# Loading all rows of the key stacks before the query stacks, for the first half of the next batch, on the SyncE queue

## The chip, the cores and the metric

The kernel runs on one core of one Trainium2 chip. The metric is device time in microseconds (us) of one execution. Three runs of the kernel before gave 1634.35, 1639.19 and 1637.96 us; their median is 1637.96. TensorE is PE here, VectorE is DVE, ScalarE is ACT, GpSimd is POOL, and SyncE is SP; SP issues nearly all DMAs.

## The reference, cut to what matters

The program is one decoder layer over 8 batches of 512 tokens of width 256, with a context of 1601 rows per batch. It has three parts, each followed by a residual sum and a layer norm. The change touches only how the operands of the second part reach their place.

```python
x = layernorm(x + self_attention_3_iterations(x))
# cross attention, 16 heads of 16 dims, 1601 context rows
q = split_heads(x @ Wq.T); k = split_heads(ctx @ Wk.T); v = split_heads(ctx @ Wv.T)
scores = einsum('bhqd,bhkd->bhqk', q, k) / sqrt(16)
scores = where(mem_mask, scores, -inf)
attn = softmax(scores, axis=-1)
x = layernorm(x + merge_heads(attn @ v) @ Wo.T)
# adapter FFN: one of 8 adapters is chosen per batch
base = x @ W_base + b_base
h = relu(x @ W_enc + b_enc); recon = h @ W_dec + b_dec
top1 = argmin(mean((recon - x) ** 2))
x = layernorm(x + base + relu(x @ W_down[top1] + b_down[top1]) @ W_up[top1] + b_up[top1])
```

## The kernel before, in words

After a front part the kernel runs one software pipeline. A batch has 4 groups of 4 heads (groups are numbered through, `m` = 4b to 4b+3 for batch b), and a group has 13 slots, one for each 128 context rows: 52 slots per batch, numbered 0 to 51. In a slot PE computes four score tiles (`pe_scores`, L1129), the product of the previous slot's probabilities with the values (`pe_values`, L1148), two pair tiles of scores for row maxima of a later group (`pe_pair`, L1089), and part of a projection job for the batch before or after (`pe_job`). ACT takes exponentials (L1267). DVE reduces the pair tiles to maxima (`dve_pair`, L1452 and L1455), evacuates jobs, and does small steps that the table `VECTOR_WORK` assigns to slots. The pair tiles have a ring of two buffers, so PE can write a pair only when DVE has read the pair two before it. Every engine works through its list in order.

The score product is made of bf16 parts. Queries and keys are split in three bf16 parts each, which are written to DRAM (`parts_dram`, `key_parts_dram`) and loaded back as stacks of 16-row blocks. Six blocks make the contraction: the three top ones (j = 0 to 2) and the three low ones (j = 3 to 5), each for two parities, so a "top" or a "low" load is 6 DMAs. The maxima of pair tiles use the top rows only and wait for the semaphore `stacked`; the full scores need the low rows too and wait for `stacked_low`. A key stack DMA moves 200.1 KB, a query stack DMA 64 KB.

The stacks hold two halves (c = 0: groups 0 and 1 of a batch; c = 1: groups 2 and 3). The half c = 0 of the next batch is loaded in the middle of the present one, after slot 25, when the scores of group 4b+1 are done: `sp_stacks(nxt, 0, m + 1)` in `sp_batch`. Seven batches do this (nxt = 1 to 7). The first user of the new top rows is a pair tile of slot 35; the first user of the low rows is slot 0 of the next batch.

Between the stacks lies `sp_spread_inverses(between)` for group 4b+1. It waits for DVE's reciprocal of the softmax sums, writes it to DRAM (L1653), waits for that write to land (L1656), and loads it back spread over 64 partitions (L1657) into `err`. In slot 33 DVE multiplies the outputs by it (the step `scale`, L1345), after a wait on the semaphore `spread`. DVE has its next pair tiles, `xk_rest` of the job `kproj` 5 (L1399) and the maxima of group 4b+3 behind that step; PE needs the pair buffers, and in slot 35 the job `loss` (L1039) waits for that `xk_rest`. The maxima go through DRAM as well (`sp_max_rows`, L1621 and L1627) and are needed by the first score of slot 39.

Of the kernel before, what the change touches and what calls it, by code (L numbers as in the profile page):

```python
# [714 lines left out]
def cross_attention_and_ffn(nc, g):  # L715

    sem, W, ident, ident_b, scores, pairs, av = g.sem, g.W, g.ident, g.ident_b, g.scores, g.max_scores, g.av
    with ExitStack() as s:
# [858 lines left out]
        def sp_key_parts_out(n):  # L1577

            for one in on["kparts_out"]:
                nc.sync.wait_ge(one, 48 * n)  # L1580
# [6 lines left out]
        def stack_row(j, par):  # L1587
            return ROW_A[par] + HD * j if j < TOP else ROW_B[par] + HD * (j - TOP)

        def sp_key_stacks(b, c, top, some=slice(0, S2)):  # L1590

            for j in range(TOP) if top else range(TOP, len(KPART)):
                src = g.kpart_dram[c, KPART[j]][:, some].rearrange("(h e d) n -> e d h n", e=2, d=HD)
                for par in range(2):
                    row = stack_row(j, par)
                    nc.sync.dma_start(kst[row:row + HD, c, :, par, some],
                                      src[par]).then_inc(on["stacked"] if top else on["stacked_low"], 16)
            if top and some.start == 0:
                for par in range(2):
                    row = R_MASK[par]  # L1600
                    nc.sync.dma_start(kst[row:row + 1, c, :, par, :],
                                      g.mask_dram[b:b + 1].unsqueeze(1).broadcast_to([1, HP, SP_])).then_inc(on["stacked"], 16)

        def sp_query_stacks(c, top, some=slice(0, T), done=None):
            for j in range(TOP) if top else range(TOP, len(QPART)):
                src = g.part_dram[c, QPART[j]][:, some].rearrange("(h e d) n -> e d h n", e=2, d=HD)
                for par in range(2):
                    row = stack_row(j, par)
                    nc.sync.dma_start(qst[row:row + HD, c, :, par, some],
                                      src[par]).then_inc(done or (on["stacked"] if top else on["stacked_low"]), 16)  # L1610
# [35 lines left out]
        def sp_spread_inverses(m):  # L1646

            sp = nc.sync
            k, these = half_rows(m)
            sp.wait_ge(inverted, m + 1)  # L1650
            if m >= 2:
                sp.wait_ge(spread, 16 * (m - 1))
            sp.dma_start(g.rsum_dram[m % 2].rearrange("j (s x) -> (j s) x", x=GH * T // P), rs[:, m % 2, :]).then_inc(rs_out, 16)  # L1653
            sp.wait_ge(rs_out, 16 * (m + 1))
            if m >= 2:
                sp.wait_ge(scaled, m - 1)  # L1656
            sp.dma_start(rsb[these, :], g.rsum_dram[m % 2].unsqueeze(1).broadcast_to([GH, HD, T])).then_inc(spread, 16)  # L1657

        def sp_stacks(b, c, between=None):

            if b:
                sp_key_parts_out(2 * (b - 1) + 1 + c)
                if c:
                    nc.sync.wait_ge(on["qparts_out"], 48 * (2 * (b - 1) + 1 + c))
            if b or c:
                before = GROUPS * b - (NG if c == 0 else 0)
                if before:
                    nc.sync.wait_ge(made, GH * XKT * before)
            if b and not c:
                sp_key_stacks(b, c, True)  # L1670
                nc.sync.wait_ge(on["qparts_out"], 48 * (2 * (b - 1) + 1 + c))
                sp_query_stacks(c, True)
                if between is not None:
                    sp_spread_inverses(between)
                sp_query_stacks(c, False)
                sp_key_stacks(b, c, False)
                return
            for top in (True, False):
                sp_query_stacks(c, top)
                if top and between is not None:  # L1680
                    sp_spread_inverses(between)
                sp_key_stacks(b, c, top)
# [30 lines left out]
        def sp_batch(b):  # L1713
# [6 lines left out]
            if prev >= 0:  # L1720
                sp_move_outputs(m - 1)
                sp_load_x1(prev)
            sp_stacks(b, 1, m - 1 if prev >= 0 else None)
            if nxt < B:
                if b:
# [16 lines left out]
            if nxt < B:  # L1742
                sp_stacks(nxt, 0, m + 1)
                sp_free_key_dram(nxt, 1)
                sp_key_parts(4, use + 4)
                if nxt + 1 < B:
                    sp_load_x(nxt + 1)
                sp_key_parts(5, use + 5)
            else:
                sp_spread_inverses(m + 1)  # L1750
# [659 lines left out]
```

## Time and profile before

| | |
|---|---|
| median of three runs | 1637.96 us (1634.35 to 1639.19) |
| the profiled execution | 1639.14 us, span 1636.6 us |
| mean granted PE clock | 0.992 |
| PE busy | 1577.6 us, 96% of the span |
| DVE busy | 1287.8 us, 79% |
| ACT busy | 1044.5 us, 64% |
| SP's DMA queue (q1) | 38.1% of 16 engines, 123.06 MB |

One batch takes about 187 us in the steady part (the same ACT step of the chain stands at 536.14 and at 723.40 us). The profiled execution is 2.5 us longer than its span, and 1.2 us longer than the median. The queue of DMAs is far from full over the whole span, but it is worked in bursts: the DMA line of the page goes from 0 to 7 tenths from slice to slice. Times of rows are from the start of the span.

### The profile page before, as it was taken

The page shows a single profiled execution, that of the slowest core. Times are in us where ns is not written, and L with a number is a line of the kernel's source. Part 1 is how long each engine was busy: PE and PEld are TensorE (multiplying, and loading weights), DVE is VectorE, ACT ScalarE, POOL GpSimd, SP SyncE. Part 2 cuts the span into 40 slices and gives each one's busy share as a digit, 9 for nine tenths or more (in the row PEclk, how much of TensorE's full clock was granted, in tenths as well). Part 3 has the DMA queues.
Part 4 walks back from the last instruction along what each step waited for, and adds up shares of the span by engine and source line. Part 5 has one row for each costly group of instructions (what it writes and reads, how often), then busy time and mean ns, then how long its engine had stood idle before and what let it go on. Part 6 is the DMA issues. An engine that isn't in the chain of part 4 may idle for free.

```text
span 1636.6 us, 25498 instructions
## 1 busy us (share of the span) xinstructions
PE 1577.6 (96%) x9560; PEld 582.7 (36%) x9560; DVE 1287.8 (79%) x1905; ACT 1044.5 (64%) x1984; POOL 162.5 (10%) x153
## 2 busy tenths in 40 slices
PE   6778999999999999999999999999999999999997
PEld 5442323332333333332334323432333323332234
DVE  5788887888789878888788877888778877887523
ACT  2226777766666676776666666666666676666661
POOL 6311000100011000100001000100001000000000
PEclk9889999999999999999999999999999999999999
DMA  5556162543417171452607152261707234160010
GB/s 157 114 137 107 60 96 54 94 108 55 98 28 140 48 119 33 84 131 36 113 16 140 63 89 64 65 115 49 128 11 117 57 55 84 50 79 5 10 33 16
DMA packets 118664, 125.21 MB, mean 77 GB/s; under 512 B 35187, under 2 KB 100340, under 8 KB 118541
## 3 DMA queue, kind: packets, MB, share of 16 engines
q1 hardware_dynamic: 117724, 123.06, 38.1%
q8 instruction: 75, 1.23, 0.3%
q10 hardware_dynamic: 816, 0.53, 0.1%
q14 instruction: 49, 0.39, 0.1%
HBM read 84.18 MB, written 35.03 MB: 73 GB/s over the span
## 4 chain that ended last, share of the span: by engine, by line
PE 88%; DVE 5%; ACT 4%; DMA 2%; issue 1%; POOL 1%; SPq 0%; POOLq 0%; DVEq 0%
PE banks L1129 24%; PE values L1148 24%; PE banks L1089 12%; PE work L1019 5%; PE work L1005 5%; PE work L964 4%; PE work L1026 3%; ACT xprobs L1267 3%; PE work L1032 3%; DVE xneg_max_pieces L1452 2%; PE work L1011 2%; PE work L1035 1%; DMA max_dram<-xneg_max_rows 1%; PE work L1044 1%; PE work L949 1%
## 5 line engine op out<-in xcount | busy, mean ns | idle before, releaser
L1267 ACT ACTIVATE xprobs<-banks 128x512 f32<-128x512 f32 x1664 | 900.6, 595 | 407.9 <-PE banks L1129 403.9
L1452 DVE TENSOR_REDUCE xneg_max_pieces<-banks 128x2 f32<-128x1024 f32 x768 | 908.5, 1218 | 209.4 <-PE banks L1089 205.6
L1129 PE MATMUL banks<-xq_stacks,xk_stacks 99*128 99x512 bf16 (+1 forms) x1664 | 518.4, 385 | 11.4 <-ACT xprobs L1267 3.5
L1148 PE MATMUL values<-xprobs,xv_rows 128*17 128x512 f32 x3328 | 437.9, 598 | 1.6 <-ACT xprobs L1267 1.6
L1129 PEld LDWEIGHTS banks<-xq_stacks,xk_stacks 99*128 99x128 bf16 (+1 forms) x1664 | 127.3, 97 | 394.9 <-ACT xprobs L1267 285.7
L1089 PE MATMUL banks<-xk_stacks,xq_stacks 49*128 49x512 bf16 (+1 forms) x2048 | 251.3, 335 | 13.9 <-DVE xneg_max_pieces L1452 11.6
L1089 PEld LDWEIGHTS banks<-xk_stacks,xq_stacks 49*128 49x128 bf16 x2048 | 57.5, 94 | 344.7 <-DVE xneg_max_pieces L1452 226.2
L1148 PEld LDWEIGHTS values<-xprobs,xv_rows 128*17 128x17 f32 x3328 | 55.1, 95 | 124.4 <-issue 118.8
L1523 POOL TENSOR_TENSOR xk_parts<-xk_rest,xk_parts 128x401 bf16<-128x401 f32 (+1 forms) x64 | 59.1, 923 | 376.3 <-ACT xk_parts L1246 376.3
L1518 POOL TENSOR_TENSOR xrstd<-xrstd,mhalf 128x4 f32<-128x4 f32 x21 | 21.2, 1012 | 594.4 <-DVE xrstd L1321 594.4
L1019 PE MATMUL work<-xvT,ctxT_a 128*128 128x128 f32 (+1 forms) x416 | 56.8, 281 | 2.0 <-DVE xk_rest L1399 1.9
L1019 PEld LDWEIGHTS work<-xvT,ctxT_a 128*128 128x128 f32 (+1 forms) x416 | 54.8, 193 | 10.9 <-issue 3.9
L1455 DVE TENSOR_REDUCE xneg_max_pieces<-banks 128x8 f32<-128x520 f32 x64 | 44.5, 695 | 17.6 <-PE banks L1089 17.4
L1026 PE MATMUL work<-x2T,wenc 128*128 128x512 f32 x112 | 57.8, 596 | 0.0
L1230 ACT ACTIVATE xk_parts<-work 128x401 bf16<-128x401 f32 (+1 forms) x64 | 32.5, 507 | 39.6 <-PE work L1005 39.6
L1528 POOL TENSOR_TENSOR xq_parts<-xq_rest,xq_parts 128x512 bf16<-128x512 f32 x15 | 17.4, 1157 | 405.4 <-ACT xq_parts L1249 405.4
L1019 PEld LDWEIGHTS work<-xvT,ctxT_b 128*128 128x128 f32 (+1 forms) x416 | 54.4, 187 | 8.7 <-ACT x2T L1192 0.8
L1032 PE MATMUL work<-x2T,wdecT 128*128 128x512 f32 x112 | 57.2, 591 | 0.0
L1019 PE MATMUL work<-xvT,ctxT_b 128*128 128x128 f32 (+1 forms) x416 | 55.4, 274 | 0.0
L1005 PE MATMUL work<-ctxT_a,xkT 128*128 128x400 f32 (+1 forms) x128 | 52.2, 528 | 0.8 <-DVE xq_rest L1413 0.8
L1337 DVE STREAM_TRANSPOSE xT<-xa 32x256 f32<-32x256 f32 x112 | 48.8, 435 | 3.3
L1005 PE MATMUL work<-ctxT_b,xkT 128*128 128x400 f32 (+1 forms) x128 | 48.2, 498 | 0.0
(299 smaller groups left out, 1040.7 us busy)
## 6 DMA issues: line engine op xcount, KB each, us to landing
xk_stacks<-key_parts_dram SPq DMA_DIRECT2D x186, 200.1 KB, 10.3
key_parts_dram<-xk_parts SPq DMA_DIRECT2D x144, 100.0 KB, 2.1
xq_stacks<-parts_dram SPq DMA_DIRECT2D x186, 64.0 KB, 5.9
ctxT_a<-in_ctxT SPq DMA_DIRECT2D x4, 1601.0 KB, 7.7
ctxT_b<-in_ctxT SPq DMA_DIRECT2D x4, 1601.0 KB, 8.0
parts_dram<-xq_parts SPq DMA_DIRECT2D x45, 128.0 KB, 1.8
key_parts_dram<-xk_parts SPq DMA_DIRECT2D x48, 100.2 KB, 9.5
xa<-in_x SPq DMA_DIRECT2D x8, 512.0 KB, 8.9
```

The costliest lines, as they stand in the source:

```text
L964: last = nc.tensor.matmul(W[:, i * D:(i + 1) * D], left, right, start=c == 0, stop=c == steps - 1)
L1005: last = pe.matmul(W[:, 0:n], xkT[:, kin, c * P:(c + 1) * P], ctx[b % 2][:, kin, k0:k0 + n], start=kin == 0, stop=kin == CH - 1)
L1019: last = pe.matmul(W[0:rows, (tt - first) * P:(tt - first + 1) * P], ctx[b % 2][:, kin, tt * P:tt * P + rows], xvT[:, kin, c * P:(c + 1) * P],
L1026: last = pe.matmul(W[:], wenc[:, kin, 2 * i:2 * i + 2, :].rearrange("p n h -> p (n h)"), x2T[:, kin, :], start=kin == 0, stop=kin == CH - 1)
L1032: last = pe.matmul(W[:], wdecT[:, kin, i * P:(i + 1) * P], x2T[:, kin, :], start=kin == 0, stop=False)
L1089: last = pe.matmul(pairs[n % MRING][:, par, at:at + w], qst[rows, k, h2, par, q * P:(q + 1) * P], kst[rows, k, h2, par, k0:k0 + w], start= ...
L1129: pe.matmul(at, kst[0:ROWS[par], k, h2, par, t * P:(t + 1) * P], qst[0:ROWS[par], k, h2, par, :], start=True, stop=True).then_inc(made, 1)
L1148: last = pe.matmul(av[32 * j:32 * j + HD + 1, :], vals[:, k, t, gr * GH + j, :], probs[:, sl % 2, j, :], start=t == 0, stop=t == XKT - 1)
L1267: nc.scalar.activation(probs[:, sl % 2, j, :], score_bank(n)[0], ACT.Exp).then_inc(exped, 1)
L1337: v.transpose(xT[32 * c:32 * (c + 1), :, :].rearrange("p k (n a i) -> p a k n i", a=P // 32, i=32)[:, a], xa[32 * a:32 * (a + 1), :, :].re ...
L1452: nc.vector.tensor_reduce(nmp[:, of % 2, :, j2, q, piece], pairs[n % MRING][:, :, :], AX.X, ALU.max, negate=True).then_inc(on["mxr"], 1)
L1523: nc.gpsimd.tensor_tensor(kpart[:, i % KBUF, 2, 0:n], krest[:, i % KBUF, 0:n], kpart[:, i % KBUF, 1, 0:n], ALU.subtract).then_inc(on["klow ...
```

## The change

In the branch of `sp_stacks` for the first half of the next batch, the six DMAs of the low key rows move from the end to the place behind the top key rows and the mask rows. They are now issued before the wait for the query parts, the top query rows, the inverses and the low query rows.

```diff
             if b and not c:
                 sp_key_stacks(b, c, True)
+                sp_key_stacks(b, c, False)
                 nc.sync.wait_ge(on["qparts_out"], 48 * (2 * (b - 1) + 1 + c))
                 sp_query_stacks(c, True)
                 if between is not None:
                     sp_spread_inverses(between)
                 sp_query_stacks(c, False)
-                sp_key_stacks(b, c, False)
                 return
```

On SP, in the middle of the first batch, the rows stand as follows; L1596 are key stacks (top, then low), L1601 mask rows, L1609 query stacks (top, then low), L1653 and L1657 the inverses out and back. The lines with a minus are before, those with a plus are now.

```order
 L1596 DMA xk_stacks<-key_parts_dram 16x4x1601 x6
 L1601 DMA xk_stacks<-mask_dram 1x4x1664 x2
-L1609 DMA xq_stacks<-parts_dram 16x4x512 x6
-L1653 DMA rsum_dram<-xrsum 128x16
-L1657 DMA err<-rsum_dram 64x1x512
-L1609 DMA xq_stacks<-parts_dram 16x4x512 x6
-L1596 DMA xk_stacks<-key_parts_dram 16x4x1601 x6
+L1596 DMA xk_stacks<-key_parts_dram 16x4x1601 x6
+L1609 DMA xq_stacks<-parts_dram 16x4x512 x6
+L1653 DMA rsum_dram<-xrsum 128x16
+L1657 DMA err<-rsum_dram 64x1x512
+L1609 DMA xq_stacks<-parts_dram 16x4x512 x6
```

Six key stack DMAs have moved ahead of fourteen others; nothing is added or removed. The lists of PE, DVE, ACT and POOL are the same in both kernels. On DVE, at the end of slot 33 and in slot 34 of a batch with an adapter job (the second batch here), this stands in both, with the semaphores that each row waits for; `x_inverses_spread` is the semaphore of L1657.

```order
326 L1441 SCALAR_TENSOR_TENSOR loss_rows<-bdec_cols,x_sums,loss_part 128x8 [waits x_own_dve]
327 L1345 TENSOR_TENSOR xo_by_dims<-xo_by_dims,err 64x512 [waits x_inverses_spread]
328 L1452 TENSOR_REDUCE xneg_max_pieces<-banks 128x2 [waits loop_max_made]
329 L1455 TENSOR_REDUCE xneg_max_pieces<-banks 128x2x4 [waits loop_max_made]
330 L1399 TENSOR_TENSOR xk_rest<-work,xk_parts 128x400 [waits loop_k_low,loop_k_high,loop_work_full]
331 L1468 TENSOR_REDUCE xneg_max<-xneg_max_pieces 128x16 [waits loop_max_read]
332 L1444 COPY l<-work 128x8 [waits loop_work_full]
```

Nothing moved on this engine; the row that waits for the inverses stands where it stood.

## Rows read from the trace of the kernel before

**Rows 1.** The page, parts 1 and 4: busy time, and the chain.

```profile
PE 1577.6 (96%) x9560; PEld 582.7 (36%) x9560; DVE 1287.8 (79%) x1905; ACT 1044.5 (64%) x1984; POOL 162.5 (10%) x153
...
PE 88%; DVE 5%; ACT 4%; DMA 2%; issue 1%; POOL 1%; SPq 0%; POOLq 0%; DVEq 0%
```

**Rows 2.** Timeline of SP's queue, third batch: start, us, line, DMA, count.

```profile
582.70 2.79 SPq L1596 DMA_DIRECT2D xk_stacks<-key_parts_dram  x6
...
586.84 2.81 SPq L1609 DMA_DIRECT2D xq_stacks<-parts_dram  x6
589.75 0.37 SPq L1653 DMA_DIRECT2D rsum_dram<-xrsum  x1
597.37 0.58 SPq L1657 DMA_DIRECT2D err<-rsum_dram  x1
597.99 2.79 SPq L1609 DMA_DIRECT2D xq_stacks<-parts_dram  x6
...
614.21 0.58 SPq L1621 DMA_DIRECT2D max_dram<-xneg_max_rows  x1
616.72 1.28 SPq L1627 DMA_DIRECT2D xq_stacks<-max_dram  x2
```

**Rows 3.** Windows: us, busy of PE, PEld, DVE, ACT, POOL, clock, DMA share, GB/s.

```profile
584.50:595.50 11.00, 11.00 (x64) 3.28 (x64) 7.52 (x10) 6.87 (x14) 0.00 (x0) 1.00 1.06 138
...
311.00:333.00 22.00, 22.00 (x147) 8.76 (x146) 20.41 (x35) 14.10 (x26) 1.01 (x1) 1.00 1.07 124
...
597.00:598.00 1.00, 1.00 (x6) 0.49 (x4) 1.00 (x1) 0.56 (x2) 0.00 (x0) 1.00 0.00 0
...
613.00:614.00 1.00, 1.00 (x4) 0.47 (x3) 0.86 (x4) 0.85 (x2) 0.00 (x0) 1.00 1.08 345
```

**Rows 4.** Line L1609 alone, the six query stacks issued at 597.99.

```profile
DMA to landing us min/median/max: 2.4/2.8/3.8
```

**Rows 5.** Timeline of DVE, third batch, end of slot 33 and slot 34.

```profile
607.59 0.69 DVE L1345 TENSOR_TENSOR xo_by_dims<-xo_by_dims,err 64x512 f32<-64x512 f32 x1
608.31 1.23 DVE L1452 TENSOR_REDUCE xneg_max_pieces<-banks 128x2 f32<-128x1024 f32 x1
609.45 0.69 DVE L1455 TENSOR_REDUCE xneg_max_pieces<-banks 128x8 f32<-128x520 f32 x1
610.54 0.58 DVE L1399 TENSOR_TENSOR xk_rest<-work,xk_parts 128x400 f32<-128x400 f32 x1 [0.40 <-issue]
```

**Rows 6.** Timeline of PE, third batch, slot 35 and the start of slot 39.

```profile
611.26 0.61 PE L1039 MATMUL work<-loss_rows,minus_two 128*128 128x8 f32 x4
...
624.77 0.62 PE L1129 MATMUL banks<-xq_stacks,xk_stacks 99*128 99x512 bf16 x2
```

**Rows 7.** Timeline of the first batch, queue, DVE and PE.

```profile
233.22 0.59 SPq L1657 DMA_DIRECT2D err<-rsum_dram  x1
...
238.27 0.69 DVE L1345 TENSOR_TENSOR xo_by_dims<-xo_by_dims,err 64x512 f32<-64x512 f32 x1
...
240.13 0.69 DVE L1455 TENSOR_REDUCE xneg_max_pieces<-banks 128x8 f32<-128x520 f32 x1
...
241.83 0.60 PE L1089 MATMUL banks<-xk_stacks,xq_stacks 49*128 49x512 bf16 x4
```

**Rows 8.** Timeline, the same two steps in the second and the seventh batch.

```profile
409.23 0.58 SPq L1657 DMA_DIRECT2D err<-rsum_dram  x1
...
420.32 0.69 DVE L1345 TENSOR_TENSOR xo_by_dims<-xo_by_dims,err 64x512 f32<-64x512 f32 x1
...
1349.45 0.58 SPq L1657 DMA_DIRECT2D err<-rsum_dram  x1
...
1357.69 0.69 DVE L1345 TENSOR_TENSOR xo_by_dims<-xo_by_dims,err 64x512 f32<-64x512 f32 x1
```

**Rows 9.** Windows of the front part, columns as in rows 3.

```profile
108.00:114.00 6.00, 1.97 (x10) 0.71 (x10) 5.86 (x9) 0.97 (x3) 1.16 (x1) 0.84 0.01 1
...
112.00:119.00 7.00, 5.31 (x24) 3.83 (x24) 4.50 (x5) 0.35 (x1) 0.00 (x0) 0.51 0.18 59
```

## The prediction

> **What bounds the kernel now.** I read the page first: PE is busy 96% of the span and makes 88% of the chain that ended last [rows 1]. So a delay of PE in the main pipeline is lost for good: there is no slack in which it could catch up. Second, the waits of each engine: in the seven loads that the change touches PE waits for nothing; in the windows of the loads it is busy in all of the time [rows 3]. An earlier arrival of the low key rows can therefore give nothing, since nobody waits for them: their first user is slot 0 of the next batch. What is left to ask is what else in SP's list now comes later, and who waits for it. Third, then, the timeline of SP's queue [rows 2], and fourth the timelines of DVE and PE where the items behind the moved DMAs are used [rows 5 to 8].
>
> **What SP's queue does at this place.** In the third batch SP issues the top key rows at 582.70 and the top query rows at 586.84. At 589.75 it issues the write of the inverses and then stands still until 597.37, when that small write (8 KB) has landed [rows 2]. It took 7.6 us because it lay in the queue behind the stacks: the queue's DMA engines are at 1.06 of their time from 584.5 to 595.5, and idle from 597 to 598 [rows 3]. So DMAs of this queue are served in the order of issue, and the landing of the inverses marks the moment at which everything issued before them has drained. Only then the spread is issued (L1657, 597.37), and DVE's multiplication that needs it ran at 607.59 [rows 2, 5]: 10.2 us after the issue.
>
> **The change part by part.**
>
> 1. The issue itself. Six DMAs cost SP 2.79 us [rows 2] wherever they stand, and their issue lies beside 12 us of draining. Cost nothing.
>
> 2. The low key rows now drain ahead of the inverses. They are 6 x 200.1 KB = 1.23 MB. The nearest rates are those of the same kind of transfer: 138 GB/s in the window of the top key and query rows, 124 GB/s where top and low key rows of the other half drain one behind the other [rows 3]. That is 8.9 to 9.9 us; I take 9.5, because key rows are what is added and they make most of the slower window. The issue of the spread in the third batch moves from 597.37 to 606.9. The Trainium skill, on the page "DMA: Bandwidth & Descriptors", section "Specifications", gives a fabric ceiling of 435 GB/s for the 16 engines. By that alone 1.23 MB would take 2.8 us, an estimate from the page; the third batch's spread would be issued at 600.2 and the change would be nearly free. The windows show a third of that rate at a DMA share above 1, so the measured rate decides.
>
> 3. The spread's own landing is not in a row. The first query stack issued behind it, at 597.99, landed after 2.4 us, at 600.4, which is 3.0 us after the spread's issue; the last of the six, issued near 600.4, landed 3.8 us later, 6.8 us after it [rows 2, 4]. I take the middle, 4.9 us, since the spread fills few, long rows beside those stacks; 3.0 and 6.8 are the ends. What follows it in the queue is the same as before.
>
> 4. DVE waits in slot 33. With 9.5 + 4.9 = 14.4 us after the old issue time of the spread, DVE's wait ends at 611.8 in the third batch instead of being over by 607.59: 4.2 us. In the first batch, whose slots 26 to 33 are short of adapter work, it ends at 247.6 against 238.27: 9.35 us [rows 7]. In the second batch 423.6 against 420.32: 3.3 us. In the seventh 1363.85 against 1357.69: 6.2 us [rows 8]. The other three batches have the same pair of rows 9.9, 10.4 and 10.4 us apart, so 4.5, 4.0 and 4.0 us.
>
> 5. What of it reaches PE. Behind L1345 DVE has the two pair tiles of slot 34 and `xk_rest` (L1399), which had 0.40 us of idle time ahead of it, ended at 611.12, and released PE's L1039, which ran at 611.26 [rows 5, 6]. PE is in order, so all but 0.40 + 0.14 = 0.54 us of DVE's wait becomes a stall of PE. In the first batch there is no L1039; there the second pair of slot 35 needs the buffer that L1455 frees (ended 240.82, against a PE start of 241.83 for the first pair and some 0.3 us more for the second [rows 7]), slack 1.25 us. PE's losses are 8.1 (first), 2.8 (second), 3.6 (third), 4.0, 3.5, 3.5 (the three like it) and 5.6 (seventh). Sum 31.1 us.
>
> 6. The top query rows land some 9.5 us later. They drained by 597.37 and are needed near 611.8, slot 35; 606.9 is still early, and in the first batch, where 242.5 meets 241.83, the longer stall of step 5 covers it. Cost nothing; without that stall it would be under 1 us once.
>
> 7. The key parts 4, the load of `xa` and the key parts 5 are issued behind, up to 4 us later. Their users are in later slots and in the next batch. Cost nothing, beside the rival on the maxima below.
>
> 8. The clock. After PE had been busy only 1.97 of 6 us in the front part the granted clock went to 0.5 and stayed near that for almost 7 us in which PE worked 5.31 us [rows 9]. The 1.2 GHz level against 2.4 GHz doubles the time of the work in it. In the first batch PE idles 8 us; I add 2 us for that batch (some 4 us of work at half clock), and nothing for the others, where the stall is 3 to 4 us between full stretches.
>
> **The sum.** 1639.14 (the profiled execution, 1636.6 of span and 2.5 around it) + 31.1 + 2 = 1672.2 us. It lies 1.2 us above the median of the runs, so I forecast **1671 us** for the median, 2.0% slower.
>
> Its ends: with 8.9 and 3.0 us in place of 9.5 and 4.9 every wait is 2.5 us shorter, seven times, so +15.6 us instead of +33: 1654. With 9.9 and 6.8 every wait is 2.3 us longer: +49, 1687.
>
> **The rivals.**
>
> A. The clock falls in every batch. Stalls of 3 to 6 us come near the gap that the front part had when the clock fell [rows 9]. For it speaks that the front part still had some matmuls in its gap; against it, that its thin stretch was 6 us long and PE here works fully on both sides. Price: some 4 us of work at half clock, 2 us, in six more batches: +12, so 1683. The Trainium skill, on the page "TensorE: Matmul & The Clock Gate", section "What's actually happening", says that the throttled state is the default and that activity releases it, so that an idle array falls back to half its clock; by that, stalls of some us are no small matter. The front part's rows agree that it falls, and cannot tell for a stall as short as these.
>
> B. The transfer is hidden. If the six stacks drained at the 345 GB/s that the queue reaches from 613 to 614 us [rows 3], with large plain loads in it, they would take 3.6 us; with a spread that lands in 3.0 us the wait ends at 604.0 in the third batch, before 607.59. Only the first batch waits (1.6 us, of which PE sees 0.3). Then the kernel is at 1638, no change. The idle stretch at 597 [rows 3], which the moved DMAs shorten, has nobody waiting at its end, so this cannot become a gain that can be measured; only luck of the queue at the maxima could bring a us or two. This is the case on the other side; it decides from the point where added drain plus landing stay under 10 us. Against it stands the measured rate of the very same transfer.
>
> C. The maxima become late too. The write of the maxima (614.21) and its load (616.72) were through by about 620, and slot 39 starts at 624.77 [rows 2, 6]: 4.8 us of slack. With PE shifted as much as DVE this slack stays; but the query stacks, key parts and `xa` are now nearer in front of that write. If it took 11 us instead of 2.5 PE would wait 4 us more per batch, 6 times: 1695. Against it: the total of bytes is the same and the stall of DVE gives the queue the same time to drain.
>
> D. Order of service. If a small write could pass the stacks in the queue, only the issue time of 2.8 us would be added and the wait would be as in B. The 7.6 us of before [rows 2] speak against it.
>
> **How the numbers follow.** Steps 1 to 8 as worked: 0.58, own range 1654 to 1687. A: 0.25. B with D: 0.07. C: 0.05. A partly hidden case between B and the forecast, +6 to +15: 0.05. The range that leaves out no more than 2 in 10 is 1650 to 1690. A difference under 0.3% (5 us) is about what a measurement of this kernel cannot tell from no change. Faster than that: 0.02. Within it: 0.06. Slower: 0.92.
>
> **What would show it.** In the profile after, SP's wait between L1653 and L1657 in the middle of a batch should be near 14 to 17 us instead of 7.6 (step 2). DVE should show a new wait, L1345 for the DMA `err<-rsum_dram`, seven times, 3 to 9 us each, 36 us in total (step 4); PE's L1039 should follow an idle time of some 3 to 4 us, and the first batch should show an L1089 after about 8 us (step 5). The granted clock should dip after the first batch's stall alone (step 8), or after each (rival A). The forecast is wrong if L1345 shows no wait: then step 2 or 3 is mis-sized, or DMAs pass each other. It is also wrong if DVE waits and PE does not, which would mean that PE has slack that I did not see.

## The result, and the profile after

The changed kernel takes 1691.9 us (median of 3 runs, 1689.56 to 1692.7) against 1637.96 us before: the ratio is 1.0326, 95% interval 1.0303 to 1.0348. That is slower by 3.3%, on the forecast side, but 1.9 us beyond the upper end of the forecast's range (1690) and 21 us above the forecast of 1671. The medians lie 53.9 us apart. The profiled execution took 1689.56 us, with a span of 1687.3 us, so the difference to be explained between the two traces is 50.7 us of span.

The chain and the waits come first. The first fence is from the page of the changed kernel: the chain by engine, and the groups that gained idle time, with what ended it (the last column).

```profile
PE 74%; DMA 10%; DVE 6%; SPq 5%; ACT 3%; issue 2%; POOL 0%; POOLq 0%; DVEq 0%; ACTq 0%
...
L1089 PE MATMUL banks<-xk_stacks,xq_stacks 49*128 49x512 bf16 (+1 forms) x2048 | 255.5, 340 | 23.4 <-DVE xneg_max_pieces L1452 20.7
```

The second is the list of waits: us in total, times, longest.

```profile
DVE xo_by_dims L1345 <- DMA err<-rsum_dram: 39.1, 7, 10.8
...
PE work L1039 <- DVE xk_rest L1399: 25.0, 6, 6.4
PE banks L1089 <- DVE xneg_max_pieces L1452: 20.7, 16, 9.3
```

In [rows 1] PE made 88% of the chain and DMA 2%. Now DMA has 10% and the queue of SP 5%. DVE waits for the spread inverses seven times, 39.1 us, where it had no such wait; PE waits 25.0 us in six batches at L1039, and 9.3 us once at L1089, 34.2 us together.

The third is the timeline of SP's queue at the same place as [rows 2].

```profile
598.75 2.79 SPq L1596 DMA_DIRECT2D xk_stacks<-key_parts_dram  x6
...
602.89 2.81 SPq L1596 DMA_DIRECT2D xk_stacks<-key_parts_dram  x6
605.75 2.77 SPq L1609 DMA_DIRECT2D xq_stacks<-parts_dram  x6
608.62 0.36 SPq L1653 DMA_DIRECT2D rsum_dram<-xrsum  x1
622.24 0.57 SPq L1657 DMA_DIRECT2D err<-rsum_dram  x1
```

From the first stack to the spread it is now 23.5 us (598.75 to 622.24), where it was 14.7 (582.70 to 597.37): 8.8 us more, for the 1.23 MB that now lie ahead. The same difference, read in each of the seven batches, is 10.7, 9.0, 8.8, 9.3, 10.4, 11.1 and 10.2 us, 9.9 on average. In the third batch the wait for the small write alone is 13.6 us from its issue, instead of 7.6.

The fourth is the timeline of DVE, the third batch (as [rows 5]) and the first (as [rows 7]); the bracket is the idle time ahead and what ended it.

```profile
251.45 0.69 DVE L1345 TENSOR_TENSOR xo_by_dims<-xo_by_dims,err 64x512 f32<-64x512 f32 x1 [10.82 <-DMA err<-rsum_dram]
...
627.08 0.69 DVE L1345 TENSOR_TENSOR xo_by_dims<-xo_by_dims,err 64x512 f32<-64x512 f32 x1 [3.46 <-DMA err<-rsum_dram]
627.79 1.23 DVE L1452 TENSOR_REDUCE xneg_max_pieces<-banks 128x2 f32<-128x1024 f32 x1
...
629.66 0.58 DVE L1399 TENSOR_TENSOR xk_rest<-work,xk_parts 128x400 f32<-128x400 f32 x1
```

The fifth is the timeline of PE: the stalls of the first, second, third and seventh batch (as [rows 6, 7]).

```profile
253.54 1.12 PE L1089 MATMUL banks<-xk_stacks,xq_stacks 49*128 49x512 bf16 x4 [9.26 <-DVE xneg_max_pieces L1452]
...
440.03 0.61 PE L1039 MATMUL work<-loss_rows,minus_two 128*128 128x8 f32 x4 [2.04 <-DVE xk_rest L1399]
...
630.29 0.88 PE L1039 MATMUL work<-loss_rows,minus_two 128*128 128x8 f32 x4 [2.90 <-DVE xk_rest L1399]
...
1409.02 1.02 PE L1039 MATMUL work<-loss_rows,minus_two 128*128 128x8 f32 x4 [6.40 <-DVE xk_rest L1399]
```

The 3.46 us of DVE become 2.90 us of PE; the 0.56 us between them are the slack that the forecast had at 0.54. L1039 itself takes 0.88 us in the third batch, against 0.61 in [rows 6]: the clock has changed. The windows of the changed kernel show it (columns as in [rows 3]; the clock is the third value from the end).

```profile
246.00:250.00 4.00, 0.00 (x0) 0.00 (x0) 0.00 (x0) 0.00 (x0) 0.00 (x0) 0.77 0.32 87
250.00:260.00 10.00, 6.46 (x22) 2.27 (x24) 6.79 (x11) 3.28 (x7) 0.94 (x1) 0.58 0.50 135
...
440.00:447.00 7.00, 6.97 (x36) 3.02 (x36) 5.95 (x14) 4.72 (x10) 1.83 (x2) 1.00 0.34 111
...
628.00:630.00 2.00, 0.00 (x0) 0.00 (x0) 1.97 (x3) 0.00 (x0) 0.00 (x0) 1.00 0.64 117
630.00:637.00 7.00, 6.71 (x20) 2.85 (x24) 3.93 (x10) 2.82 (x6) 0.94 (x1) 0.53 0.29 95
...
613.00:620.50 7.50, 7.50 (x41) 2.33 (x40) 5.39 (x5) 5.09 (x10) 0.00 (x0) 1.00 1.05 137
```

After the third batch's stall PE is busy again (6.71 of 7 us) at a granted clock of 0.53, near the 1.2 GHz level. The same follows every stall but the second batch's, which has 1.00 behind it. Two of the stretches at the lower level, with their ends set more closely, behind the third and the seventh stall:

```profile
630.50:637.30 6.80, 6.80 (x20) 2.64 (x23) 3.83 (x9) 2.89 (x7) 0.94 (x1) 0.50 0.22 70
...
1409.00:1415.50 6.50, 6.48 (x20) 2.92 (x24) 3.28 (x8) 2.44 (x5) 0.94 (x1) 0.50 0.11 33
```

Read in this way, PE's work at the lower level behind the first and the third to seventh stall is 4.86, 6.80, 3.40, 3.40, 4.20 and 6.48 us, 29.1 us in all. If it would have taken half as long at the full clock, it cost 14.6 us; this is an estimate from these windows.

**The account.** The first write of inverses (L1653) stood at 176.02 us before and stands at 178.40 us now; ahead of it the two kernels are the same. In the traces of the experiments below the same step stands anywhere from 172.1 to 176.4 us, so the 2.4 us are put down to differences from run to run. From there to the end it was 1636.6 - 176.0 = 1460.6 us and is 1687.3 - 178.4 = 1508.9 us: 48.3 us more. Of these 34.2 us are PE's idle time in the seven stalls, and 14.1 us are left. The windows gave 14.6 us for the lower clock without this subtraction, so the account closes within 0.5 us.

### The profile page after: what moved, and what is told of

It is laid out like the page before. It is cut to its first block, busy times and chain, and to the rows that moved or that the text cites. A ratio compares the mean times of both kernels' runs of the same rounds, so it can differ in the third digit from the quotient of the medians.

```text
span 1687.3 us, 25498 instructions
## 1 busy us (share of the span) xinstructions
PE 1594.4 (94%) x9560; PEld 587.9 (35%) x9560; DVE 1287.6 (76%) x1905; ACT 1044.8 (62%) x1984; POOL 161.7 (10%) x153
## 3 DMA queue, kind: packets, MB, share of 16 engines
q8 instruction: 75, 1.23, 0.3%
## 4 chain that ended last, share of the span: by engine, by line
PE 74%; DMA 10%; DVE 6%; SPq 5%; ACT 3%; issue 2%; POOL 0%; POOLq 0%; DVEq 0%; ACTq 0%
PE banks L1129 20%; PE values L1148 19%; PE banks L1089 10%; DMA rsum_dram<-xrsum 6%; PE work L1019 6%; PE work L1005 5%; PE work L964 4%; DVE xneg_max_pieces L1452 3%; ACT xprobs L1267 3%; SPq L1596 2%; DMA err<-rsum_dram 2%; PE work L1026 2%; PE work L1032 2%; PE work L1011 2%; SPq L1609 1%
## 5 line engine op out<-in xcount | busy, mean ns | idle before, releaser
L1129 PE MATMUL banks<-xq_stacks,xk_stacks 99*128 99x512 bf16 (+1 forms) x1664 | 522.1, 387 | 11.2 <-ACT xprobs L1267 3.5
L1089 PE MATMUL banks<-xk_stacks,xq_stacks 49*128 49x512 bf16 (+1 forms) x2048 | 255.5, 340 | 23.4 <-DVE xneg_max_pieces L1452 20.7
L1129 PEld LDWEIGHTS banks<-xq_stacks,xk_stacks 99*128 99x128 bf16 (+1 forms) x1664 | 127.8, 97 | 398.4 <-ACT xprobs L1267 282.9
L1089 PEld LDWEIGHTS banks<-xk_stacks,xq_stacks 49*128 49x128 bf16 x2048 | 57.6, 94 | 355.8 <-DVE xneg_max_pieces L1452 217.3
L1246 ACT ACTIVATE xk_parts<-xk_rest 128x401 bf16<-128x401 f32 (+1 forms) x64 | 34.7, 542 | 47.9 <-DVE xk_rest L1399 47.2
L1019 PE MATMUL work<-xvT,ctxT_a 128*128 128x128 f32 (+1 forms) x416 | 60.2, 292 | 1.8 <-DVE xk_rest L1399 1.8
L1528 POOL TENSOR_TENSOR xq_parts<-xq_rest,xq_parts 128x512 bf16<-128x512 f32 x15 | 17.3, 1156 | 406.5 <-ACT xq_parts L1249 406.5
L1005 PE MATMUL work<-ctxT_b,xkT 128*128 128x400 f32 (+1 forms) x128 | 53.2, 541 | 0.0
```

The costliest lines, as they stand in the source:

```text
L1005: last = pe.matmul(W[:, 0:n], xkT[:, kin, c * P:(c + 1) * P], ctx[b % 2][:, kin, k0:k0 + n], start=kin == 0, stop=kin == CH - 1)
L1019: last = pe.matmul(W[0:rows, (tt - first) * P:(tt - first + 1) * P], ctx[b % 2][:, kin, tt * P:tt * P + rows], xvT[:, kin, c * P:(c + 1) * P],
L1089: last = pe.matmul(pairs[n % MRING][:, par, at:at + w], qst[rows, k, h2, par, q * P:(q + 1) * P], kst[rows, k, h2, par, k0:k0 + w], start= ...
L1129: pe.matmul(at, kst[0:ROWS[par], k, h2, par, t * P:(t + 1) * P], qst[0:ROWS[par], k, h2, par, :], start=True, stop=True).then_inc(made, 1)
```

## The experiments

All are the changed kernel with the edit shown; "..." stands for lines left out. Theory T throughout: the inverses stand in the queue behind the low key rows, DVE waits for them in slot 33, PE waits for DVE, and the clock falls behind most of the stalls. The ratios are to the kernel before, run beside them.

**The inverses back ahead of the low key rows.**

```diff
             if b and not c:
                 sp_key_stacks(b, c, True)
-                sp_key_stacks(b, c, False)
                 nc.sync.wait_ge(on["qparts_out"], 48 * (2 * (b - 1) + 1 + c))
                 sp_query_stacks(c, True)
                 if between is not None:
                     sp_spread_inverses(between)
+                sp_key_stacks(b, c, False)
                 sp_query_stacks(c, False)
```

> The changed kernel, but with the low key rows behind the top query rows and the inverses, and still ahead of the low query rows. Theory T (the inverses stand in the queue behind 1.2 MB of low key rows, DVE waits for them in slot 33, PE waits for DVE, and the clock falls after each long stall): the inverses are where they were before, so no wait at L1345 and a time of 1638 us, within 5 us. Rival R (the key rows ahead of the query rows crowd the queue, and the top query rows, the maxima or the key parts come late): low key rows are still ahead of the low query rows, and part of the loss stays, over 10 us. A time near 1690 would leave both without a cause.

Measured: 1638.31 us, ratio 1.0002 (0.9992 to 1.0011). The group of L1345 in this kernel, in the list of groups (busy, mean ns, then idle time ahead and what ended it):

```profile
L1345 DVE TENSOR_TENSOR xo_by_dims<-xo_by_dims,err 64x512 f32<-64x512 f32 x31 | 21.2, 683 | 0.9 <-DMA err<-rsum_dram 0.4
```

0.4 us of waits are left of 39.1. That the low key rows are ahead of the low query rows costs nothing; the whole loss hangs on their being ahead of the top query rows and the inverses. Which of these two matters this run cannot say, since both are back ahead of them; the next one can.

**The step that waits, moved to a later slot.**

```diff
-            28: [("invert", "o", 1, NOW)], 33: [("scale", "o", 1, NOW)],
+            28: [("invert", "o", 1, NOW)], 38: [("scale", "o", 1, NOW)],
```

> The changed kernel, with DVE's step that waits for the inverses of group 4b+1 (scale, L1345) moved from slot 33 to slot 38; SP's order stays as changed. Theory T: everything that the change delays still comes as late, but nobody waits: the spread lands about 5 us after its issue, 3 to 11 us after the old place of the step, and slot 38 is 15 us after it. PE idle before L1039 goes from 25.0 us to under 2 us, no dips of the clock in the loop, time 1638 to 1642 us. Rival R (top query rows, maxima or key parts are late): the time stays above 1650.

Measured: 1640.54 us, ratio 1.0002 (0.9989 to 1.0016). SP's order is that of the changed kernel, the spread comes just as late, and the loss is gone. From the list of groups and the list of waits of this kernel:

```profile
L1345 DVE TENSOR_TENSOR xo_by_dims<-xo_by_dims,err 64x512 f32<-64x512 f32 x31 | 21.2, 683 | 0.5
...
PE banks L1089 <- DMA xq_stacks<-parts_dram: 3.4, 2, 2.0
```

The second row is step 6 of the forecast: with the stall gone, the top query rows are 2.0 us late in the first batch. The other 1.4 us of the row stand in the front part, where the kernel before has such a wait too. The transfers, the burst and the other items of SP that come later cost no more than that, and rival R is out. This settles that the path from L1345 to PE carried the loss, the clock included, up to those 2 us.

**Four of six, and two of six.**

```diff
-                sp_key_stacks(b, c, False)
+                sp_key_stacks(b, c, False, these=range(TOP, TOP + 2))   # TOP + 1 for two of six
                 ...
                 sp_query_stacks(c, False)
+                sp_key_stacks(b, c, False, these=range(TOP + 2, len(KPART)))   # TOP + 1 for two of six
```

The new argument `these` names the parts j that the call loads.

> The changed kernel with four of the six low key DMAs (j = 3 and 4) ahead, and two (j = 5) at the old place. Theory T: some 3.2 us less in front of the inverses, so the waits of DVE (10.8, 2.6, 3.5, 4.4, 5.0, 5.9, 7.0 us) shrink by that each: 7.6, 0, 0.3, 1.2, 1.8, 2.6, 3.8. PE stalls about 6 us in the first batch and 7 in the others, and the clock falls after the two or three longest: +16 to +20 us, 1654 to 1658. Rival L (the loss is a fixed price of any wait, or goes with the number of bytes): +36, two thirds of the loss, 1674.

Measured: 1655.8 us, ratio 1.0098 (1.0071 to 1.0124), where T said 1654 to 1658. Rival L is out. DVE's waits are 6.42, 2.66, 1.19, 2.53, 1.17, 2.17 and 3.44 us, 19.6 in all. T had 17.3 in all, but nothing in the second batch and 1.2 in the fourth, so it was off by more than 1 us in three batches. PE idles 4.85 us at L1089 and 9.8 us at L1039. The timeline of PE in the second and sixth batch, and the windows behind:

```profile
431.55 0.61 PE L1039 MATMUL work<-loss_rows,minus_two 128*128 128x8 f32 x4 [2.10 <-DVE xk_rest L1399]
...
1188.44 0.61 PE L1039 MATMUL work<-loss_rows,minus_two 128*128 128x8 f32 x4 [1.61 <-DVE xk_rest L1399]
```

```profile
432.00:436.00 4.00, 4.00 (x24) 1.45 (x25) 3.44 (x8) 2.53 (x6) 0.95 (x1) 1.00 0.61 193
...
1189.00:1192.50 3.50, 3.50 (x10) 1.58 (x10) 2.83 (x6) 1.08 (x2) 0.95 (x1) 0.52 0.63 194
```

The clock stayed up after 2.10 us of idle time and fell after 1.61 us. The length of the stall alone does not decide it. The profiled execution is the slowest of the four (1660.78 us). In it the clock fell behind four stalls (first, fourth, sixth and seventh batch), where T had two or three, and windows as above give some 9.5 us for it. With 14.7 us of stalls this makes the 24 us by which this trace is longer than that of the kernel before, counted from the first write of inverses. So the median inside T's range does not confirm the single terms: for the profiled execution T's sum was 4 us too small.

> The changed kernel with two of the six low key DMAs (j = 3) ahead and four at the old place. Theory T: some 6.3 us less in front of the inverses than in the changed kernel; DVE's waits are 4.5 us in the first batch, about 0.6 in the seventh and 0 elsewhere; PE stalls about 3 us once, with or without a dip of the clock (up to 2 us): 1641 to 1644 us. Rival L (loss in proportion to the bytes moved ahead): a third of 52 us, 1656.

Measured: 1642.56 us, ratio 1.0013 (0.9992 to 1.0034). DVE waits 3.41 us in the first batch and 0.15 us in the fourth, nothing elsewhere. So 0, 2, 4 and 6 DMAs ahead give about 0, 4 (within its uncertainty), 17 and 54 us: no price by the byte, but a threshold in each batch. With two ahead, one batch passes it clearly and a second by 0.15 us; with four and with six, all seven do. Rival L is out here too.

**The first batch only.**

```diff
-                sp_key_stacks(b, c, False)
+                if b == 1:
+                    sp_key_stacks(b, c, False)
                 ...
                 sp_query_stacks(c, False)
+                if b > 1:
+                    sp_key_stacks(b, c, False)
```

> The changed order for the first of the seven loads only, the old order for the other six. Theory T: the first batch alone loses its 9.3 us of stall and 2.4 us of low clock, and nothing after it: 1650 us, within 3. Rival S (the first load's lateness is passed on to the later ones, or the loads' losses are not separate): clearly more than 1653 or, if the first batch's shift were given back later, under 1645.

Measured: 1648.84 us, ratio 1.0052 (1.0036 to 1.0068), 10 us above the runs beside it. DVE waits once, 9.2 us, and PE 7.6 us at L1089. T said 1650. What this batch loses stays lost, and no later batch waits at L1345, so rival S is out and adding the losses of the batches is right.

**PE kept at work in the stall.** In slot 35, ahead of the job `loss`, PE gets matmuls with zero weights that add nothing to the values' sums.

```diff
+        FILL = {2: 11, 3: 15, 4: 18, 5: 22, 6: 27}
         ...
+            if m % GROUPS == 2 and t == 9 and m // GROUPS in FILL:
+                nc.tensor.wait_ge(nothing_in, 1)
+                for _ in range(FILL.get(m // GROUPS, 0)):
+                    nc.tensor.matmul(av[0:HD + 1, :], nothing[:], ident_b[:].unsqueeze(1).broadcast_to([P, 4, P]),
+                                     start=False, stop=False)
             if short:
                 pe_job(MAIN, short)
```

> The changed kernel, with PE kept at work in the stall of slot 35 of the third to seventh batch: 11, 15, 18, 22 and 27 extra matmuls (17 by 128 weights of zero, 512 columns, added to the values' sums, so nothing changes) ahead of L1039, 0.2 us each, 0.5 us less in all than the stalls of 2.9 to 6.4 us. Theory T with the clock: the stalls stay, but the granted clock does not fall in those five batches, and the 11 us that those dips cost come back: 1680 us. Rival N (the dips cost nothing, all of the loss is stall): 1690 or above.

Measured: 1675.72 us, ratio 1.0231 (1.0208 to 1.0253): 16 us faster than the changed kernel, although PE was given work, and 4 us faster than T said. The three windows are of this kernel, behind the stalls of the second, third and fourth batch:

```profile
439.00:446.00 7.00, 7.00 (x26) 2.35 (x25) 5.60 (x12) 4.13 (x8) 0.90 (x1) 0.76 0.35 113
...
626.00:633.00 7.00, 5.67 (x31) 2.53 (x26) 5.09 (x11) 2.16 (x5) 0.95 (x1) 1.00 0.74 190
817.00:824.00 7.00, 7.00 (x39) 2.99 (x30) 5.60 (x11) 2.50 (x6) 0.95 (x1) 1.00 0.61 175
```

Where PE was filled (third batch on) the clock stays at 1.00; where it was not (the second batch, idle 2.88 us here) it falls, to 0.76 over the stretch. Rival N is out: the low clock was a loss of its own. Its size follows from the two traces, counted from the first write of inverses (L1661 here, at 174.98 us): 1497.2 us here against 1508.9, so 11.7 us less. DVE's waits are 4.5 us shorter (34.6 us against 39.1), but from the fourth batch on the extra matmuls ran longer than the stall and held up the job `loss` (L1041 here), by 3.4 us in all. This is PE in the seventh batch, the longest case; `xk_rest` had ended at 1394.59:

```profile
1390.90 5.99 PE L1173 MATMUL values<-ident_b,nothing 128*17 128x512 bf16 x27
1396.83 0.61 PE L1041 MATMUL work<-loss_rows,minus_two 128*128 128x8 f32 x4
```

So the delays of PE are 1.1 us shorter in all, and 10.6 us are left for the clock, near the 11 us that T gave. Why DVE's waits were shorter here is open.

**The inverses on ACT's queue.** SP's order as changed; the write is issued by ACT at the start of slot 30, the spread at the start of slot 32.

```diff
+            if m % GROUPS == 2 and m // GROUPS + 1 < B and t in (4, 6):
+                of = m - 1
                 ...
+                if t == 4:
+                    nc.scalar.wait_ge(inverted, of + 1)
                     ...
+                    nc.scalar.dma_start(g.rsum_dram[of % 2].rearrange("j (s x) -> (j s) x", x=GH * T // P),
+                                        rs[:, of % 2, :]).then_inc(rs_out, 16)
+                else:
+                    nc.scalar.wait_ge(rs_out, 16 * (of + 1))
                     ...
+                    nc.scalar.dma_start(rsb[these, :], g.rsum_dram[of % 2].unsqueeze(1).broadcast_to([GH, HD, T])
+                                        ).then_inc(spread, 16)
...
-                sp_stacks(nxt, 0, m + 1)
+                sp_stacks(nxt, 0)
```

> The changed order on SP, but the two DMAs of the inverses of group 4b+1 are issued by ACT on its own queue, the write at the start of slot 30 and the spread at the start of slot 32. Theory Q (the small write is late because DMAs of one queue are served in the order of issue): on another queue the write lands in about 2 us although the stacks are still draining, the spread is there before slot 33 ends, no wait at L1345, 1638 to 1642 us. Rival E (the 16 DMA engines are simply full, and any transfer waits some 10 us whatever its queue): ACT itself would then wait in slot 32 for the write and hold up the exponentials, and the time is 1690 or more.

Measured: 1693.09 us, ratio 1.0326 (1.0287 to 1.0364), no better than the changed kernel, and where rival E had it. DVE no longer waits at L1345, but only because ACT waits in its place, 48.7 us in the seven batches, and PE then waits for ACT's exponentials at L1129. The first row is the landing time of the seven writes, from the list of line L1279 of this kernel; the others are ACT's timeline in the third batch.

```profile
DMA to landing us min/median/max: 13.7/14.8/15.9
```

```profile
604.40 0.32 ACTq L1279 DMA_DIRECT2D rsum_dram<-xrsum  x1
...
619.20 0.53 ACTq L1285 DMA_DIRECT2D err<-rsum_dram  x1
619.83 1.09 ACT L1267 ACTIVATE xprobs<-banks 128x512 f32<-128x512 f32 x2 [6.32 <-DMA rsum_dram<-xrsum]
```

Theory Q is wrong. An 8 KB write on a queue that holds nothing else lands after 14.8 us in the median. All that time the stacks issued by SP are draining. Two views of the DMA queues of this kernel, third batch, show what the two queues moved after the write's issue at 604.40; q1 is SP's, q10 ACT's (packets, MB, share of 16 engines). The first row is from 604.5 to 613.8 us, where q10 moved nothing; the others are from 613.8 to 618.0 us.

```profile
q1 hardware_dynamic: 462, 1.18, 103.5%
...
q1 hardware_dynamic: 296, 0.53, 100.9%
q10 hardware_dynamic: 144, 0.01, 6.0%
```

So the write was not begun for over 9 us and took some 5 us more. It landed 0.8 us before the last of the key stacks that SP had issued ahead of it. What the forecast had right is the moment, which is about when what was issued before has drained; by which queue it was issued made little difference. Its words "DMAs of this queue are served in the order of issue" were too narrow, though they gave the right number. Why an empty queue gave the write no turn is open.

## Why the prediction was wrong, step by step

- **Step 1, issue is free:** right.
- **Step 2, the drain:** 9.5 us forecast for every batch. Measured are 8.8 us in the third, just under the bounds of 8.9 to 9.9, but 10.7, 10.4, 11.1 and 10.2 us in the first and the three last, over them. The average of 9.9 us is a rate of 124 GB/s, that of the slower window. This term was too small by 3 us over the seven batches.
- **Step 3, the spread's landing:** 4.9 us forecast from bounds of 3.0 and 6.8. DVE starts 4.84 us after the spread's issue (622.24 to 627.08), and 4.6 to 5.1 us after it in the others. Right.
- **Step 4, DVE's wait:** seven waits, 39.1 us, against 35.6 (the terms as they stand in the forecast, which says 36 at its end). By batch 10.8, 2.6, 3.5, 4.4, 5.0, 5.9 and 7.0 us against 9.35, 3.3, 4.2, 4.5, 4.0, 4.0 and 6.2. The first batch and the three last are 0.8 to 1.9 us longer. These are the batches with the longer drain; without a wait DVE would still have come to L1345 within 0.2 us of the old spacing.
- **Step 5, what reaches PE:** the slack of 0.54 us was 0.56 us. PE's stalls are 34.2 us against 31.1; the excess comes from step 4 and so from step 2.
- **Step 6, the top query rows:** right in that the stall covers them. Seen bare, with L1345 moved, they cost 2.0 us once, where the step said under 1.
- **Step 7, the rest of SP's list:** right; the maxima went out at 633.72 in the third batch and their load followed at 635.70, so rival C did not come.
- **Step 8, the clock, is the step that failed.** It gave 2 us to the first batch and nothing to the others, because their stalls of 3 to 4 us (5.6 in the seventh, by its own step 5) stand between full stretches. The trace has a low clock after six of the seven stalls, 14.1 us in all by the account above and 14.6 by the windows; filling five stalls gave back 10.6 us, although the clock then fell in the second batch, where it had not before. Of the stalls that the step priced at nothing, five in six were followed by a low clock, so full work on both sides did not protect them. Rival A had the mechanism and the size (2 us a batch, 14 in all, time 1683) and was given only 0.25. It said every batch, and the second escaped. With it the sum is 1639 + 31 + 14 = 1684.
- **What is left** between 1684 and the profiled 1689.56 us is 3 us of longer stalls (from step 2) and 2.4 us of a later start of the loop.
- **The range** reached only 1690 since the wide ends of steps 2 and 3 were set against a sum without rival A. Both had to be added: the rival's 12 us were a price on top, not a case beside.

The Trainium skill's page "TensorE: Matmul & The Clock Gate", section "What's actually happening", has activity release the throttle; the low clock behind six stalls and the filled stalls without it agree. The fabric ceiling that the Trainium skill gives, page "DMA: Bandwidth & Descriptors", section "Specifications", was no guide to this transfer: the drain ran at 137 GB/s with a DMA share of 1.05.

## What to carry to other kernels

A small DMA that an in-order engine waits for must not be issued behind bulk that nobody waits for yet; its lateness is the bulk's drain time, which can be read from how long such a small write already waits. Another issuing queue did not rescue it here. Count what is left of the old spacing batch by batch, because the price is a threshold and not a rate. And when a stall opens in a TensorE that was always busy, add the slow clock behind it to the price: here it was 14 us on top of 34, in seven stalls of 2 to 9 us.

## What the runs showed of the hardware beyond that

A write of 8 KB on ACT's queue took 13.7 to 15.9 us to land while stacks issued by SP drained. In the third batch it landed 22.2 us after the first stack's issue (597.00 to 619.20). That is hardly sooner than the 23.5 us of the changed kernel, where it was queued on SP, with the top query rows ahead of it as well; here only the first of those six had been issued before it.

The granted clock fell after a PE stall of 1.61 us (0.52 over the next 3.5 us), after one of 1.97 us in the same kernel and, with two of six DMAs ahead, after one of 1.84 us. It stayed at 1.00 after stalls of 1.98 us (with L1345 moved), 2.04 us (the changed kernel) and 2.10 us (four of six). This is the window behind the stall of 1.84 us:

```profile
245.50:249.00 3.50, 3.50 (x10) 1.13 (x12) 3.07 (x6) 2.08 (x5) 0.95 (x1) 0.54 1.05 204
```

What separates these cases was not settled.
